# Fewer matmul signals in a graph layer: which matmuls signal, who waits for them, and wider column rings

## Chip, cores and metric

The kernel runs on one core of one Trainium2 chip. The time is device time in microseconds, median of three runs. The profile is of one separate execution.

## The reference

A graph transformer layer on N = 6250 nodes with F = 256 features and E = 106250 edges (50000 random pairs in both directions and a self loop for each node):

```python
xn = layernorm(x)
# gnn: twice  out = segment_mean(segment_mean((h @ W)[src], dst)[dst], src) + b, with prelu between
x = x + gnn(xn, edges, W1, b1, W2, b2, a) + mix(xn, Wqkv, Wout, bout)   # linear attention, 8 heads of 64
x = x + ffn(layernorm(x), ...)                                           # 8 experts, top 2, 256 -> 512 -> 256
```

Each segment mean takes for each edge the row of one end (1 KB), sums the rows by the other end, and divides by the count.

## The kernel before

Every segment sum is a pass over the edges, sorted by target block of 128 nodes (`NB` = 49 blocks) and padded to `NC` = 880 chunks of 128 edges. There are four passes (p = 0 to 3), each of `TURNS` = 55 turns of `U` = 16 chunks. In each chunk:

- ACT copies the row numbers of four chunks (`IB` = 4) to `idxb` (`row_numbers`, L616), after it has waited for `s_mm`, the matmuls of the same four slots one turn before.
- POOL issues one indirect DMA a chunk (`gather_pass`, L492) into one of 16 slots of `gbuf`. It waits for `idxb` every four chunks and for `s_mm` of its slot each time; `settle` before each is a semaphore instruction of POOL.
- PE (`product_pass`, L1281) multiplies the one-hot matrix of the chunk's targets (`ohg`) with the gathered rows into one of four PSUM banks (`AB` = 4). It waits for the gather (`s_g`) and for the bank (`s_acc`), and each matmul signals `s_mm`. The operands are fp32, and the trace shows two weight loads and two matmuls for one.
- DVE adds the bank to the accumulator of the chunk's block (`add_chunk`, L916) and signals `s_acc`; twice a turn it makes the one-hots of eight chunks (`one_hots`, L921), after `s_mm`.

The edges are sorted on the chip, once by dst (o = 0) and once by src (o = 1). In a sort, each of `EC` = 832 columns of edges (one edge per partition) becomes two one-hots on DVE (`sort_column`: `ohc` of 880 and `ohs` of 128, L839 and L840), two scaled copies on ACT (`ohv`, L606 and L607), and four f16 matmuls of 128x440 on PE (L1249), which accumulate in PSUM banks 0 to 3. The rings `ohc`, `ohs` and `ohv` hold four columns, and the last of the four matmuls of each column signals `s_used`, for which DVE waits before it fills a slot again (L838). Sort 0 does its first 384 columns by 384 indirect DMAs of POOL (`scatter`, L501) and its last 448 on DVE, ACT and PE, beside DVE's counting and placing for sort 1. Sort 1's 832 columns go beside pass 0, one for each chunk: DVE makes column k + 3 (`LEAD`), then the add of chunk k; PE does chunk k, then column k.

Beside pass 1 runs the attention's key and value part (`kv_body`, L1306 and L1296, one of 49 blocks a turn), beside pass 2 its output (`mix_body`, L1343). Between passes DVE divides by the counts and SP stores the next table. After pass 3 come the norm, the router and the experts. The order of the instructions on each engine is written out by hand, so each engine is a queue in which a waiting instruction holds all behind it.

Of the kernel before, what the change touches and what calls it, by code (L numbers as in the profile page):

```python
# [17 lines left out]
P = 128  # L18
# [30 lines left out]
def gps_layer(nc, x, src, dst, gnn_w1, gnn_b1, gnn_w2, gnn_b2, gnn_a, wqkv, wout, bout,  # L49
# [25 lines left out]
    LEAD = 3  # L75
# [19 lines left out]
    with ctx:  # L95
# [51 lines left out]
        def carve(base, sizes):  # L147

            views, at = {}, 0
            for name, (shape, dt) in sizes.items():  # L150
# [9 lines left out]
                if len(shape) == 3:  # L160
# [16 lines left out]
            "fa0": ((EC,), f32), "fb0": ((EC,), f32), "ohc": ((4, NC), f16), "ohs": ((4, P), f16),  # L177
            "ohv": ((8, P), f16), "unp": ((NC,), i32)})
# [9 lines left out]
        ohc, ohs, ohv = r["ohc"], r["ohs"], r["ohv"].rearrange("p (k f) n -> p k f n", f=2)  # L188
# [21 lines left out]
                    for at in (0, KT * 2 * INNER + 2 * PAIRS * F)]  # L210
# [37 lines left out]
        s_oh, s_ohs, s_used, s_sorted, s_idx = [[sem(f"{n}{o}") for o in range(2)]  # L248
                                                for n in ("s_oh", "s_ohs", "s_used", "s_sorted", "s_idx")]
# [198 lines left out]
        def _(pool):  # L448
# [70 lines left out]
            pool.wait_ge(s_wkv, 1)  # L519
# [57 lines left out]
        def _(act):  # L577
# [25 lines left out]
            def sort_column(o, i, k):  # L603
                c = i * U + k
                act.wait_ge(s_oh[o], (i - sort_from[o]) * U + (k + 1))
                A(ohv[:, k % 4, 0, :], ohs[:, k % 4, :], ACT.Copy, scale=field_a[o][:, ds(c, 1)])  # L606
                A(ohv[:, k % 4, 1, :], ohs[:, k % 4, :], ACT.Copy, scale=field_b[o][:, ds(c, 1)]).then_inc(s_ohs[o], 1)  # L607
# [115 lines left out]
        def _(dve):  # L723
# [194 lines left out]
            def one_hots(p, i, h):  # L918

                dve.wait_ge(s_mm[p], i * U + (8 * h + 8))  # L920
# [23 lines left out]
            def inverse(p):  # L944
                dve.wait_ge(s_acc[p], NC + AB)
# [77 lines left out]
            dve.wait_ge(s_acc[3], NC + AB)  # L1023
# [174 lines left out]
        def _(pe):  # L1198
# [13 lines left out]

            def count(o):
# [4 lines left out]
                MM(PS[:, bank, 64:64 + NB], ones[:, :], rowtot[:, 0:NB], start=True, stop=True).then_inc(s_cnt[o], 1)  # L1218
# [20 lines left out]
            def open_sort(o):  # L1239
                zero = [MM(PS[:, 2 * f + h, 0:HC], z16[:, :], iota_c[:, 0:HC], start=True, stop=False)  # L1240
                        for f in range(2) for h in range(2)]
                for m in zero:
                    m.then_inc(s_used[o], 1)

            def sort_column(o, i, k):
                pe.wait_ge(s_ohs[o], (i - sort_from[o]) * U + (k + 1))
                for f in range(2):
                    for h in range(2):
                        m = MM(PS[:, 2 * f + h, 0:HC], ohv[:, k % 4, f, :], ohc[:, k % 4, h * HC:(h + 1) * HC],  # L1249
                               start=False, stop=False)  # L1250
                m.then_inc(s_used[o], 1)

            def close_sort(o):
                for f in range(2):
                    for h in range(2):
                        m = MM(PS[:, 2 * f + h, 0:HC], z16[:, :], iota_c[:, 0:HC], start=False, stop=True)
                m.then_inc(s_sorted[o], 1)
# [13 lines left out]
            def product_pass(p, start, end, body=None):  # L1271
                if start == 0:
                    pe.sem_inc(s_mm[p], U)
                    pe.sem_inc(s_acc[p], AB)
                with pe.Fori(start, end) as i:
                    for k in range(U):
# [3 lines left out]
                        pe.wait_ge(s_acc[p], i * U + (k + 1))  # L1280
                        MM(PS[:, 4 + k % AB, 0:FC], ohg[:, k, :], gbuf[:, k, :], start=True, stop=True).then_inc(s_mm[p], 1)  # L1281
# [17 lines left out]
            def kv_body(i, k):  # L1299
                if k in (3, 5):  # L1300
# [4 lines left out]
                    for kt in range(KT):  # L1305
                        m = MM(PS[:, h, :], mx["xt"][:, kt, :], mx["wkv"][:, kt, h * INNER:(h + 1) * INNER],  # L1306
# [160 lines left out]
```

## Time and profile before

| | us |
|---|---|
| median of 3 runs | 6714.9 |
| lowest, highest | 6711.88, 6718.19 |
| span of the profiled execution, first to last instruction | 8262.6 |

The profiled execution is far longer than the timed ones. Nothing is given of it outside its span. In its views "idle before <- X" names what ended a wait; "remote" and "another core or an unknown queue" mean that the profile has no record of the update that ended it; DVEq is DVE's sequencer (register and semaphore instructions).

### The profile page before, as it was taken

What the parts mean: (1) busy time and instruction counts of PE and PEld (TensorE: products, weight loads), DVE (VectorE), ACT (ScalarE), POOL (GpSimd) and SP (SyncE); (2) the same over time, 40 slices, a digit from 0 to 9 for tenths busy, and PEclk for the clock granted to TensorE, in tenths of its full rate; (3) what the DMA queues carried; (4) which work ended last, traced back from release to release, by engine and by line L of the source; (5) the groups of instructions that cost most, each with busy time, mean ns of one, the idle gap of its engine ahead of it and who ended that gap; (6) DMA issues with size and microseconds to landing.
All of it is one profiled execution on the core that took longest, in us unless ns stands there. A gap on an engine that the chain in (4) does not pass through costs nothing. (4 is left out here: it accounts for less than half of the span.)

```text
span 8262.6 us, 93487 instructions
## 1 busy us (share of the span) xinstructions
PE 4799.4 (58%) x16274; PEld 2762.7 (33%) x16275; DVE 3919.4 (47%) x9146; ACT 1396.4 (17%) x4207; POOL 4241.7 (51%) x4243
## 2 busy tenths in 40 slices
PE   3111776666666664666666355555456555554896
PEld 2000333333333332434443233333232322334564
DVE  8411995455445444444444444444433333366323
ACT  2100553333333330000000000000000000000242
POOL 0467003444444445666666466666667666632342
PEclk6555997778777786777776667776666666666898
DMA  4000001222222224333333334444543333331114
GB/s 166 14 0 0 2 0 51 60 60 60 60 60 60 58 61 116 88 91 90 90 92 87 98 113 116 118 115 114 123 135 91 88 90 89 89 76 38 39 62 132
DMA packets 330989, 639.10 MB, mean 77 GB/s; under 512 B 81808, under 2 KB 201444, under 8 KB 330448
## 3 DMA queue, kind: packets, MB, share of 16 engines
q0 software_dynamic: 191808, 490.67, 22.1%
q1 hardware_dynamic: 131396, 140.16, 5.2%
q10 hardware_dynamic: 7756, 7.97, 0.3%
q8 instruction: 8, 0.13, 0.0%
q14 instruction: 21, 0.17, 0.0%
HBM read 551.49 MB, written 87.01 MB: 77 GB/s over the span
## 5 line engine op out<-in xcount | busy, mean ns | idle before, releaser
L492 POOL DMA_INDIRECT gbuf<-table,idxb x3520 | 3508.1, 997 | 2884.0 <-ACT idxb L616 1692.0
L1281 PE MATMUL PS<-gbuf,ohg 128*128 128x257 f32 x7040 | 2732.1, 511 | 1755.0 <-issue 1004.0
L916 DVE TENSOR_TENSOR acc<-acc,PS 128x257 f32 x3520 | 1482.8, 421 | 2506.0 <-remote 964.2
L1281 PEld LDWEIGHTS PS<-gbuf,ohg 128*128 128x128 f32 x7040 | 1520.2, 242 | 2883.1 <-issue 1688.3
L1249 PE MATMUL PS<-region 128*128 128x440 f16 x5120 | 1272.6, 383 | 1159.3 <-ACT region L607 774.6
L1249 PEld LDWEIGHTS PS<-region 128*128 128x128 f16 x5120 | 502.1, 104 | 1779.0 <-ACT region L607 926.6
L616 ACT COPY idxb<-idx 128x4 int32 (+1 forms) x884 | 167.7, 191 | 3323.2 <-PE PS L1281 1960.6
L839 DVE TENSOR_SCALAR region<-iota_c,acc 128x880 f16<-128x880 f16 x835 | 395.0, 473 | 703.3 <-remote 571.5
L921 DVE TENSOR_TENSOR ohg<-iota,dl 128x1024 f32<-128x1024 f16 x444 | 545.0, 1227 | 81.5 <-issue 55.1
L606 ACT ACTIVATE region<-region,acc 128x128 f16<-128x128 f16 x835 | 335.2, 401 | 1230.0 <-DVE region L840 983.5
L501 POOL DMA_INDIRECT scattered_d<-acc x384 | 369.8, 963 | 142.7 <-issue 129.1
L839 DVE TENSOR_SCALAR region<-iota_c,region 128x880 f16<-128x880 f16 x448 | 216.7, 484 | 471.1 <-remote 432.4
L607 ACT ACTIVATE region<-region,acc 128x128 f16<-128x128 f16 x835 | 322.0, 386 | 0.0
L606 ACT ACTIVATE region<-region 128x128 f16<-128x128 f16 x448 | 177.5, 396 | 750.9 <-DVE region L840 478.5
L782 DVE TENSOR_TENSOR_SCAN region<-region,small 128x832 f32<-128x832 f16 x112 | 220.2, 1966 | 7.0
L573 POOL DMA_INDIRECT ye_d<-gbuf,fs x108 | 106.3, 984 | 221.5 <-ACT gbuf L710 205.5
L840 DVE TENSOR_SCALAR region<-iota_h,acc 128x128 f16<-128x128 f16 x835 | 211.7, 254 | 0.0
L1419 PE MATMUL PS<-region,ohg 128*128 x436 | 207.8, 600 | 0.0
L1442 PE MATMUL PS<-acc,gbuf 128*128 x864 | 204.1, 379 | 0.0
L1306 PE MATMUL PS<-region 128*128 128x512 f32 x392 | 196.9, 627 | 0.0
L1442 PEld LDWEIGHTS PS<-acc,gbuf 128*128 128x128 f32 x864 | 164.4, 190 | 68.1 <-issue 51.6
L607 ACT ACTIVATE region<-region 128x128 f16<-128x128 f16 x448 | 172.8, 386 | 0.0
(262 smaller groups left out, 3094.0 us busy)
## 6 DMA issues: line engine op xcount, KB each, us to landing
gbuf<-table,idxb POOLq DMA_INDIRECT x3520
table<-acc SPq DMA_DIRECT2D x21, 896.0 KB, 6.7
region<-xt_d SPq DMA_DIRECT2D x98, 128.0 KB
gbuf<-ye_d SPq DMA_DIRECT2D x12, 1024.0 KB, 7.9
xpad_d<-acc SPq DMA_DIRECT2D x1, 6272.0 KB, 20.0
xn_d<-acc SPq DMA_DIRECT2D x49, 128.0 KB, 1.7
xt_d<-acc SPq DMA_DIRECT2D x49, 128.0 KB, 1.7
table<-acc SPq DMA_DIRECT2D x49, 128.0 KB, 1.7
```

The source lines that it names most:

```text
L492: gp.indirect_dma_start(gbuf[:, k, 0:F], None, tables[p], bass.IndirectOffsetOnAxis(idxb[:, k:k + 1], 0)).then_inc(s_g[k], 16)
L501: gp.indirect_dma_start(scattered_d, bass.IndirectOffsetOnAxis(ln["places"][:, h, k:k + 1], 0), ln["edges"][:, h, k:k + 1], None).then_inc ...
L606: A(ohv[:, k % 4, 0, :], ohs[:, k % 4, :], ACT.Copy, scale=field_a[o][:, ds(c, 1)])
L607: A(ohv[:, k % 4, 1, :], ohs[:, k % 4, :], ACT.Copy, scale=field_b[o][:, ds(c, 1)]).then_inc(s_ohs[o], 1)
L782: link.mark(V.tensor_tensor_scan(run, oh16[:, k, :], oh16[:, k, :], base[:, ds(b, 1)], ALU.add, ALU.bypass))
L839: TS(ohc[:, k % 4, :], iota_c[:, :], chunk_of[o][:, ds(c, 1)], None, ALU.is_equal)
L840: TS(ohs[:, k % 4, :], iota_h[:, :], slot_of[o][:, ds(c, 1)], None, ALU.is_equal).then_inc(s_oh[o], 1)
L916: TT(a, a, PS[:, 4 + k % AB, 0:FC], ALU.add).then_inc(s_acc[p], 1)
L921: TT(ohg[:, 8 * h:8 * h + 8, :], iota_1[:, :].unsqueeze(1).broadcast_to([P, 8, P]), dl[p % 2][:, ds(i * U + 8 * h, 8)].unsqueeze(2).broadc ...
L1249: m = MM(PS[:, 2 * f + h, 0:HC], ohv[:, k % 4, f, :], ohc[:, k % 4, h * HC:(h + 1) * HC], start=False, stop=False)
L1281: MM(PS[:, 4 + k % AB, 0:FC], ohg[:, k, :], gbuf[:, k, :], start=True, stop=True).then_inc(s_mm[p], 1)
L1442: m = MM(PS[:, 6 + k % 2, 0:F], fe["hT"][:, k % 2, t * P:(t + 1) * P], fa_["w2"][:, ds(es[k], 1), t, :].rearrange("p a f -> p (a f)"), sta ...
```

## The change

Of each two chunks (`GP` = 2) only the last matmul signals `s_mm`. In sort 0, one column in four (`SG` = 4) signals `s_used`; in sort 1 none does, and DVE no longer waits there (the adds' waits keep the order). POOL waits once per four gathers, for the adds `s_acc` of the four slots one turn before, in place of `s_mm` each time; ACT's copies of row numbers wait for `s_acc` too; `one_hots` waits for neither. PE waits for the banks once per pair. The column rings hold eight columns and `ohc`, `ohs` are separate for the two sorts; sort 1 leads by six columns. Single signals of PE elsewhere stand on a drain instruction behind the matmul. The setting of the ones in `gbuf` waits for the end of sort 0.

```diff
+    GP = 2
+    RING = 8
+    SG = 4
-    LEAD = 3
+    LEAD = 6
...
@@ gather_pass (POOL)
                         if k % IB == 0:
                             pool.wait_ge(s_idxb[p], i * (U // IB) + (k // IB + 1))
-                        pool.wait_ge(s_mm[p], i * U + (k + 1))
-                        settle(pool)
+                            pool.wait_ge(s_acc[p], i * U + (k + IB))
+                            settle(pool)
...
-            pool.wait_ge(s_wkv, 1)
+            pool.wait_ge(s_sorted[0], 1)
             gp.memset(gbuf[:, :, F:FC], 1.0).then_inc(s_zero, 1)
...
@@ row_numbers (ACT)
-                act.wait_ge(s_mm[p], i * U + (IB * h + IB))
+                act.wait_ge(s_acc[p], i * U + (IB * h + IB))
...
@@ sort_column (DVE)
-                dve.wait_ge(s_used[o], (i - sort_from[o]) * U + (k + 1))
-                TS(ohc[:, k % 4, :], iota_c[:, :], chunk_of[o][:, ds(c, 1)], None, ALU.is_equal)
-                TS(ohs[:, k % 4, :], iota_h[:, :], slot_of[o][:, ds(c, 1)], None, ALU.is_equal).then_inc(s_oh[o], 1)
+                if o == 0 and k % SG == 0:
+                    dve.wait_ge(s_used, (i - SC_FROM) * (U // SG) + (k // SG + 1))
+                TS(ohc[o][:, k % RING, :], iota_c[:, :], chunk_of[o][:, ds(c, 1)], None, ALU.is_equal)
+                TS(ohs[o][:, k % RING, :], iota_h[:, :], slot_of[o][:, ds(c, 1)], None, ALU.is_equal).then_inc(s_oh[o], 1)
...
@@ add_chunk and one_hots (DVE)
-                dve.wait_ge(s_mm[p], i * U + (U + k + 1))
-                dve.wait_ge(s_acc[p], i * U + (k + AB))
+                if k % GP == 0:
+                    dve.wait_ge(s_mm[p], i * (U // GP) + (k // GP + 1))
+                dve.wait_ge(s_acc[p], i * U + (U + k))
...
-                dve.wait_ge(s_mm[p], i * U + (8 * h + 8))
...
@@ PE
+            def signal(semaphore):
+
+                pe.drain().then_inc(semaphore, 1)
...
-                m.then_inc(s_used[o], 1)
+                if o == 0 and k % SG == SG - 1:
+                    m.then_inc(s_used, 1)
...
-                        pe.wait_ge(s_acc[p], i * U + (k + 1))
-                        MM(PS[:, 4 + k % AB, 0:FC], ohg[:, k, :], gbuf[:, k, :], start=True, stop=True).then_inc(s_mm[p], 1)
+                        if k % GP == 0:
+                            pe.wait_ge(s_acc[p], i * U + (U + k + GP - AB))
+                        m = MM(PS[:, 4 + k % AB, 0:FC], ohg[:, k, :], gbuf[:, k, :], start=True, stop=True)
+                        if k % GP == GP - 1:
+                            m.then_inc(s_mm[p], 1)
...
@@ kv_body, and in the same way count, close_sort, dots' last and mix_body
                     if h == 1:
-                        m.then_inc(s_kv, 1)
+                        signal(s_kv)
```

## Rows read from the trace of the kernel before

**Rows 1.** The page: busy time of each engine.
```profile
PE 4799.4 (58%) x16274; PEld 2762.7 (33%) x16275; DVE 3919.4 (47%) x9146; ACT 1396.4 (17%) x4207; POOL 4241.7 (51%) x4243
```

**Rows 2.** Windows: span; busy PE, PEld, DVE, ACT, POOL; PE clock, DMA, GB/s.
```profile
830.00:1283.00 453.00, 323.28 (x1552) 137.35 (x1552) 447.24 (x1049) 251.31 (x779) 5.25 (x2) 0.97 0.00 1
1283.00:3156.00 1873.00, 1228.80 (x5076) 683.95 (x5076) 915.25 (x2639) 597.38 (x1883) 851.70 (x880) 0.79 0.23 61
3199.00:4551.00 1352.00, 870.75 (x2543) 530.34 (x2543) 633.20 (x1376) 102.21 (x315) 887.53 (x881) 0.73 0.33 90
4641.00:5946.00 1305.00, 742.94 (x1934) 428.62 (x1934) 541.33 (x1122) 41.77 (x216) 873.30 (x880) 0.69 0.41 112
5983.00:7275.00 1292.00, 739.51 (x1749) 383.29 (x1749) 491.18 (x984) 41.97 (x217) 894.37 (x880) 0.65 0.35 98
7275.00:8262.00 987.00, 681.58 (x2754) 490.04 (x2754) 460.71 (x1311) 238.03 (x490) 304.09 (x264) 0.80 0.22 69
```

**Rows 3.** Timeline, a column of sort 0 beside the scatter.
```profile
341.86 0.39 ACT L607 ACTIVATE region<-region 128x128 f16<-128x128 f16 x1
342.30 1.65 PE L1249 MATMUL PS<-region 128*128 128x440 f16 x4 [7.59 <-issue]
349.30 0.96 POOL L501 DMA_INDIRECT scattered_d<-acc  x1 [0.30 <-issue]
350.46 0.45 DVE L839 TENSOR_SCALAR region<-iota_c,region 128x880 f16<-128x880 f16 x1 [8.19 <-remote]
```

**Rows 4.** Line L501: durations in ns, first and last start.
```profile
L501 POOL DMA_INDIRECT scattered_d<-acc x384: 952/958/1225, 289.8 to 822.1; - x192
```

**Rows 5.** Windows of L839 alone: DVE busy (x columns), PE clock.
```profile
285.00:300.00 15.00, 3.86 (x8) 0.66 0.02 2
300.00:830.00 530.00, 28.10 (x56) 0.50 0.02 0
```

**Rows 6.** Waits between 830 and 1283 us: total, times, longest.
```profile
PEld PS L1240 <- DVE idx L862: 14.3, 1, 14.3
```

**Rows 7.** Timeline, gathers of passes 0 and 2: start, duration, idle before.
```profile
1307.07 0.95 POOL L492 DMA_INDIRECT gbuf<-table,idxb  x1 [0.30 <-issue]
5644.60 0.95 POOL L492 DMA_INDIRECT gbuf<-table,idxb  x1 [0.30 <-issue]
```

**Rows 8.** Waits in pass 0.
```profile
POOL gbuf L492 <- ACT idxb L616: 1211.1, 102, 447.9
DVE region L839 <- remote: 571.5, 100, 7.3
```

**Rows 9.** Pass 0: timeline of PE and DVE, and the window 1293 to 1297.
```profile
1293.74 0.60 PE L1281 MATMUL PS<-gbuf,ohg 128*128 128x257 f32 x2
1294.92 0.60 PE L1281 MATMUL PS<-gbuf,ohg 128*128 128x257 f32 x2
1296.53 0.91 PE L1249 MATMUL PS<-region 128*128 128x440 f16 x4
1308.55 0.45 DVE L839 TENSOR_SCALAR region<-iota_c,acc 128x880 f16<-128x880 f16 x1 [8.70 <-issue]
1293.00:1297.00 4.00, 4.00 (x22) 2.60 (x21) 0.62 (x2) 0.69 (x2) 2.84 (x3) 1.00 0.36 102
```

**Rows 10.** Timeline of DVE, pass 0 without waits, one-hots, adds of pass 2.
```profile
1313.12 0.42 DVE L916 TENSOR_TENSOR acc<-acc,PS 128x257 f32 x1
1313.97 0.42 DVE L916 TENSOR_TENSOR acc<-acc,PS 128x257 f32 x1
1315.67 1.22 DVE L921 TENSOR_TENSOR ohg<-iota,dl 128x1024 f32<-128x1024 f16 x1
5653.91 0.42 DVE L916 TENSOR_TENSOR acc<-acc,PS 128x257 f32 x1 [0.21 <-DVE acc L916]
```

**Rows 11.** Chain of waits in pass 3: start, us, what.
```profile
6631.96 0.06 DVEq L916
6636.13 0.71 DVEq L913
```

More of the change, by code:

```diff
@@ L247, in gps_layer @@
         s_bwd, s_bwr = [[sem(f"{n}{o}") for o in range(2)] for n in ("s_bwd", "s_bwr")]
-        s_oh, s_ohs, s_used, s_sorted, s_idx = [[sem(f"{n}{o}") for o in range(2)]
-                                                for n in ("s_oh", "s_ohs", "s_used", "s_sorted", "s_idx")]
+        s_oh, s_ohs, s_sorted, s_idx = [[sem(f"{n}{o}") for o in range(2)] for n in ("s_oh", "s_ohs", "s_sorted", "s_idx")]
+        s_used = sem("s_used")
         s_stat, s_sd, s_ln, s_xn, s_xt, s_xtc, s_t1, s_t1c, s_lnd, s_lnfree, s_xpad = [
@@ L944, in inverse @@
             def inverse(p):
-                dve.wait_ge(s_acc[p], NC + AB)
+                dve.wait_ge(s_acc[p], NC + U)
                 link(TS(inv[:, :], accs[p % 2][:, :, F], 1.0, None, ALU.max))
@@ L1022, in _ @@
             acc_pass(3, 0, TURNS)
-            dve.wait_ge(s_acc[3], NC + AB)
+            dve.wait_ge(s_acc[3], NC + U)
             V.memset(z16[:, 0:1], 0.0).then_inc(s_fin, 1)
@@ L1217, in count @@
                 MM(PS[:, bank, 0:NB], lower[:, :], rowtot[:, 0:NB], start=True, stop=True)
-                MM(PS[:, bank, 64:64 + NB], ones[:, :], rowtot[:, 0:NB], start=True, stop=True).then_inc(s_cnt[o], 1)
+                MM(PS[:, bank, 64:64 + NB], ones[:, :], rowtot[:, 0:NB], start=True, stop=True)
+                signal(s_cnt[o])
             pe.wait_ge(s_wkvc, 2)
@@ L1239, in open_sort @@
             def open_sort(o):
-                zero = [MM(PS[:, 2 * f + h, 0:HC], z16[:, :], iota_c[:, 0:HC], start=True, stop=False)
-                        for f in range(2) for h in range(2)]
-                for m in zero:
-                    m.then_inc(s_used[o], 1)
+                for f in range(2):
+                    for h in range(2):
+                        MM(PS[:, 2 * f + h, 0:HC], z16[:, :], iota_c[:, 0:HC], start=True, stop=False)
+                if o == 0:
+                    pe.sem_inc(s_used, RING // SG)
             def sort_column(o, i, k):
@@ L1255, in close_sort @@
                     for h in range(2):
-                        m = MM(PS[:, 2 * f + h, 0:HC], z16[:, :], iota_c[:, 0:HC], start=False, stop=True)
-                m.then_inc(s_sorted[o], 1)
+                        MM(PS[:, 2 * f + h, 0:HC], z16[:, :], iota_c[:, 0:HC], start=False, stop=True)
+                signal(s_sorted[o])
             pe.wait_ge(s_bw[0], 1)
@@ L1272, in product_pass @@
                 if start == 0:
-                    pe.sem_inc(s_mm[p], U)
-                    pe.sem_inc(s_acc[p], AB)
+                    pe.sem_inc(s_acc[p], U)
                 with pe.Fori(start, end) as i:
@@ L1319, in _ @@
             dots()
-            MM(PS[:, 2, :], z16[:, :], iota_c[:, 0:512], start=False, stop=True, skip_group_check=True).then_inc(s_dots, 1)
+            MM(PS[:, 2, :], z16[:, :], iota_c[:, 0:512], start=False, stop=True, skip_group_check=True)
+            signal(s_dots)
             product_pass(1, NB, TURNS)
@@ L1342, in mix_body @@
                     for kt in range(KT):
-                        m = MM(PS[:, 0, 0:F], mx["xt"][:, kt, :], gmat[:, kt, :], start=kt == 0, stop=kt == KT - 1)
-                    m.then_inc(s_mix, 1)
+                        MM(PS[:, 0, 0:F], mx["xt"][:, kt, :], gmat[:, kt, :], start=kt == 0, stop=kt == KT - 1)
+                    signal(s_mix)
             pe.sem_inc(s_mix, 1)
```

19 lines of the change are left out of this document (10 added, 9 removed).

## Prediction

> **What bounds the kernel now.** I read the page first: no engine is busy for more than 58% of the span [rows 1], so no engine's work explains it; it is made of waits. The windows by stage then show where time goes [rows 2]: four passes of 880 gathers each, of 1873, 1352, 1305 and 1292 us, are 5822 of 8262 us. The reader is to see that POOL's busy time is nearly the same in all four (852 to 894 us) while their length is not.
>
> The timeline gives POOL's own pace: a gather takes 0.95 us and the next one starts 0.30 us later, 1.25 us apart, with nothing to wait for [rows 7]. 880 of them are 1100 us, 20.0 us a turn. So every pass exceeds what POOL needs, by 773, 252, 205 and 192 us. The waits of pass 0 say what POOL lacks there: row numbers from ACT, 1211 us (448 of which lie before the first gather) [rows 8]. ACT copies them when PE's matmuls have signalled.
>
> Next I asked whether PE is late or its signal. In the timeline of sort 0, PE has its four matmuls of a column issued by about 343.9 us, and DVE, which only waits for a free slot of four, goes on at 350.46, after 8.19 us idle, with "remote" as releaser; ACT to PE takes 0.05 us in the same place [rows 3]. In pass 0, PE issues without a gap up to 1297.4, and then stands; DVE's next column starts at 1308.55, after 8.70 us idle [rows 9]. POOL goes on issuing through both. What is late is the update from a matmul to its waiter, and it is late while POOL issues indirect DMAs; from 830 to 1283 us, where POOL does nothing, DVE is busy 447 of 453 us [rows 2]. This is an inference: the releaser has no record.
>
> **The sum against the profiled execution.** Without late signals, the start would be as follows. Only 64 of the 448 columns are done by 830 us [rows 5]. From there to 1283 us DVE does the last 384 with counting and placing in 453 us, 1.18 us each [rows 2]; all 448 would take 528 us from 290 on, to 818. The scatter goes on to 823 whatever DVE does [rows 4], and about 14 us of unpacking follow [rows 6], with a few for the read back: first gather at 840 instead of 1283, 443 us less. So:
>
> 840 (start) + 4 x 1100 (gathers) + 43 + 90 + 37 (between passes) + 987 (rest) = 6397 us.
>
> The profiled span, 8263, is 1866 above it. The median of the timed runs, 6714.9, is 318 above it. The two differ by 1548 us for the same program. So at most about a sixth (318 of 1866) of these stalls exists in a timed run. That the profile itself stretches the kernel is seen on DVE's sequencer as well: in pass 3 the same kind of register instruction takes 0.06 us and, 4 us later, 0.71 [rows 11]. I therefore take the shape of the stalls from the trace and their size from the median. If sort 0 had none of the 318 us, the passes of a timed run would be 7% above POOL's pace (318 / 4400).
>
> **The change part by part.**
>
> Signals removed. Pass 0 loses 24 of 32 PE signals a turn, the other passes 8 of 16, sort 0 three of four. If delivery is a matter of how many, half to three quarters of the 318 us goes; if none of the 318 us is late signals, 0 goes. Both ends stay: 0 and 318. I take 60%, because pass 0 and sort 0, which lose three quarters, hold 1216 of the profile's 1866 us, and because a late signal of a pair still holds two chunks. That is -191 us.
>
> The signals' cost to PE's own issue: at the full clock, 2.4 GHz, a chunk and a column with their two signals repeat every 1.18 us, PE busy 4.00 of 4 us [rows 9], 18.8 us a turn, under POOL's 20.0. So it is covered by POOL: 0.
>
> A page of the Trainium skill, "TensorE: Matmul & The Clock Gate", section "The cost: per-tile semaphore tail", says that increments on consecutive matmuls serialize at about 26 ns each and that one on the last is enough. By it 2928 fewer signals (4800 before, 1872 after) are an estimated 77 us at most, if none were covered; the sum would then be 6641 instead of 6527. The trace shows no gap of that kind, and the page has no delay of 8 us.
>
> Fewer instructions on POOL: a `settle` and a register wait leave three of four gathers. The scatter, which has neither between its DMAs, has the same 0.30 us between two [rows 3, 7]. Worth 0; if it did not hold, 3520 x 0.30 would be the far bound, and that is a rival below.
>
> Gathers and row numbers behind the adds: the longer chain is gather landed, pair of matmuls, add, copy, gather. A slot has 16 gathers of 1.25 us, 20.0 us, before it is needed; a group of four must be done after 13 of them, 16.3 us. Added is one pair's second chunk (1.25) and four adds, each with a column in pass 0, 0.85 us apart when DVE has no wait [rows 10]: 3.4 us. That leaves about 11 us for landing, matmul and signal. Cost 0 as long as a signal is no later than that; otherwise the second rival.
>
> Pairs of banks: PE waits for the two adds of the pair before last instead of a single one four back. It has one pair, 2.36 us at full clock [rows 9], for two adds with a column, 1.7 us, plus signals; the one-hots of eight chunks (1.22 us) can make PE wait [rows 10], but POOL gives 1.2 us a turn of cover. 0, at most 1 us in each of 55 turns.
>
> Drains: one in each of 49 turns of passes 1 and 2. PE is idle 481 and 562 us there [rows 2], which hides them; without cover, 98 x 0.6 us (the time of one chunk's matmuls [rows 9]) is 59 us. 0. Three more columns ahead of pass 0: 3 x 0.85 = 3 us on the path. Memset of the ones after sort 0: under the 14 us of unpacking, 0.
>
> Sum: 6714.9 - 191 + 3 = 6527, I say 6530 us. The same for the profiled execution, where signals are the larger part: between 30% and 60% of 1866 gone, a span of 7150 to 7700.
>
> **Rivals.**
>
> *Nothing to gain.* The late updates belong to the profiled execution alone, and the 318 us is something else (PE at its lower clock, gathers that land late). For: 1548 of 1866 us are known to be absent from timed runs. Against: something stretches them by 318, and the profile shows nothing else that delays POOL. Time 6718, 3 us over the median.
>
> *The adds hold the gathers.* When signals come late and together, ACT today copies four row numbers at once and POOL starts at once. After the change POOL starts only when DVE has added all four, 3.4 us later in pass 0: 55 x 3.4 = 187 us, and up to 2.5 us a turn in the others (4 x 0.63) [rows 10]. It decides from a delay of 11 us on. The trace has such waits, since POOL's stops in pass 0 are 14 us a turn (773 / 55). Against: fewer signals should be less late. In full, 6900; at half its price, 6810.
>
> *Much more.* If the timed gather is faster than the traced one, say 1.15 us, the floor is 6045 and the excess 670; 60% of that makes 6315. For: sequencers are slower under the profiler. Against: the pitch is the same with and without instructions between, which says that it is not theirs.
>
> **Numbers.** Forecast (50 to 290 us less) 0.52; nothing 0.15; adds hold the gathers 0.20; much more 0.13. The forecast's own range is 6425 to 6665. The range over all, 6340 to 6790, cuts off the far halves of the last two. A difference under 0.2% (13 us) is what a measurement of this kernel can't tell from none; so faster 0.65, same 0.15, slower 0.20.
>
> **What would show it.** In the profile after: in sort 0 beside the scatter, more than 56 columns by 830 us and the first gather well before 1283; in pass 0, fewer and shorter idle times of L839 and of POOL, a pass under 1500 us; POOL's pitch still 1.25 us. If the gap between two gathers shrinks, the term I set to 0 was wrong. If POOL waits for `s_acc` with DVE's adds running at 0.85 us each before it, the second rival holds. If the profiled span falls by hundreds of microseconds and the median does not, the first one does. The forecast fails if the 318 us isn't late signals.

## The result, and the profile after

| | before | after |
|---|---|---|
| median | 6713.4 us (4 runs) | 6779.9 us (4 runs) |
| lowest to highest | 6709.4 to 6718.2 | 6779.3 to 6783.8 |
| profiled execution, time / span | span 8262.6 | 6779.9 / 6778.1 |

The ratio is 1.0097, 95% interval [1.0083, 1.0112]: the change makes the kernel 66 us slower. The forecast was 6530 us, faster.

The profiled execution of the changed kernel is as short as its timed ones, while that of the kernel before is 1548 us longer than the timed ones. The experiments below say why: the kernel takes 6711 to 6715 us on some chips (kind A here) and 8251 to 8443 us on others (kind B), timed or profiled alike. By its length the result above is of kind A, the trace of the kernel before of kind B. So [rows 2] and what follows lie stage by stage beside each other, but the difference is mostly that of the chips. (A kind is a name for what a chip showed during these runs. One chip of kind B was met twice and was the same both times; no chip was seen in both kinds. Whether the cause lies in the chip itself isn't shown.)

The page: busy time of each engine, then the groups of POOL's gathers and DVE's one-hots (busy us, mean ns | idle before).

```profile
PE 5097.9 (75%) x16274; PEld 2646.6 (39%) x16275; DVE 3884.1 (57%) x9152; ACT 1398.4 (21%) x4213; POOL 4432.6 (65%) x4243
...
L497 POOL DMA_INDIRECT gbuf<-table,idxb x3520 | 3571.9, 1015 | 1223.5 <-issue 1008.8
...
L927 DVE TENSOR_TENSOR ohg<-iota,dl 128x1024 f32<-128x1024 f16 x444 | 541.6, 1220 | 0.0
```

Windows of the changed kernel by stage (columns as in [rows 2]): scatter and sort 0, the end of the scatter, the four passes, the rest.

```profile
290.00:500.00 210.00, 161.03 (x770) 68.47 (x771) 207.10 (x542) 125.96 (x386) 162.44 (x151) 0.98 0.02 1
500.00:800.00 300.00, 214.81 (x1032) 88.44 (x1029) 299.76 (x661) 168.22 (x511) 246.28 (x172) 1.00 0.01 0
800.00:956.00 156.00, 1.65 (x4) 0.43 (x4) 22.91 (x35) 4.32 (x16) 107.68 (x112) 0.50 0.02 3
956.00:2155.00 1199.00, 1131.61 (x5075) 603.67 (x5076) 883.21 (x2641) 594.83 (x1882) 917.21 (x880) 0.98 0.35 96
2203.00:3360.00 1157.00, 945.87 (x2537) 489.72 (x2537) 626.30 (x1372) 102.71 (x315) 889.15 (x881) 0.78 0.37 104
3452.00:4583.00 1131.00, 856.84 (x1940) 405.58 (x1940) 539.32 (x1127) 41.96 (x217) 863.10 (x881) 0.72 0.46 130
4622.00:5791.00 1169.00, 980.06 (x1744) 420.19 (x1744) 481.75 (x979) 41.97 (x217) 901.15 (x880) 0.56 0.37 108
5791.00:6778.00 987.00, 683.78 (x2759) 489.48 (x2758) 464.42 (x1315) 238.24 (x490) 304.21 (x264) 0.79 0.22 69
```

Read POOL's column (the fifth engine). In [rows 2] a pass was 192 to 773 us longer than 1100 us because POOL stood; here the passes are only 31 to 99 us longer, and POOL's busy time is higher than the 832.5 us that 880 gathers of 0.946 us take (the median of e18's gathers). The missing time lies inside the gathers. The timeline shows where (start, duration, [idle before]):

```profile
5030.80 1.22 DVE L927 TENSOR_TENSOR ohg<-iota,dl 128x1024 f32<-128x1024 f16 x1
5031.21 1.64 POOL L497 DMA_INDIRECT gbuf<-table,idxb  x1 [0.30 <-issue]
```

This gather, issued while DVE makes one-hots, lasts until 0.83 us after they end (5032.85 against 5032.02), 1.64 us in place of 0.95. In pass 3 this meets two of 16 gathers in each turn. The moment that decides follows from the two durations: 0.95 - 0.83 = 0.12 us after the gather's start. In the trace of pass 3, one-hots are running at that moment in 109 of the 880 gathers. Each of these ends 0.83 us after the one-hots (to 0.03 us), or after its own 0.95 us where that is later. The other 771 take 0.95 us, and none of them more than 1.05.

The scatter is lengthened too. Line L506 (durations in ns, first and last start, to be laid beside [rows 4]):

```profile
L506 POOL DMA_INDIRECT scattered_d<-acc x384: 953/977/2484, 289.1 to 930.5; - x192
```

Windows of that line alone, ahead of sort 1's placing, beside it, and behind it:

```profile
289.00:400.00 111.00, 80.03 (x82) 0.97 0.02 1
410.00:810.00 400.00, 311.82 (x205) 0.99 0.01 0
810.00:932.00 122.00, 86.87 (x91) 0.50 0.02 0
```

The timeline, DVE's wait for the end of the scatter:

```profile
936.06 7.74 DVE L858 TENSOR_SCALAR idx<-ohg 128x880 int32<-128x880 int32 x1 [131.88 <-DMA ohg<-scattered_d]
```

Sort 0's columns are now done in time: DVE makes 438 of them between 300 and 830 us, where [rows 5] has 56. But beside them DVE scans and selects for sort 1, and there a scatter DMA takes 1.52 us on the mean (311.82 / 205) in place of 0.98 before and 0.95 after. All but 1 us of this excess lies in DMAs that ran beside a scan (1.94 us) or a predicated copy (1.08 us) of that selection, not in those beside sort 0's columns alone. The scatter ends 108 us later than in [rows 4], and DVE, done at about 804 us, waits 132 us for it. The first gather is issued at 955.9 us.

By stage the span is 956 (start) + 1199 + 1156 + 1130 + 1169 (passes, first to last gather) + 48 + 93 + 40 (between) + 987 (rest) = 6778 us. The forecast's floor had 840 + 4400 + 170 + 987 = 6397. The 381 us between them are: 116 up to the first gather (108 of it the stretched scatter; the forecast's 17 us from the scatter's end to the first gather are 25), 254 in the passes, 11 between them. In the passes, POOL's DMAs that last longer than 0.946 us make 242 us (3571.9 - 4 x 832.5), and 14 us are waits in pass 0 (e4 below). No late signal of PE appears among them.

### The profile page after: what moved, and what is told of

Its sections match the earlier page's. It is cut to its first block, busy times and chain, and to the rows that moved or that the text cites. A ratio compares the mean times of both kernels' runs of the same rounds, so it can differ in the third digit from the quotient of the medians.

```text
span 6778.1 us, 84181 instructions
## 1 busy us (share of the span) xinstructions
PE 5097.9 (75%) x16274; PEld 2646.6 (39%) x16275; DVE 3884.1 (57%) x9152; ACT 1398.4 (21%) x4213; POOL 4432.6 (65%) x4243
## 4 chain that ended last, share of the span: by engine, by line
POOL 25%; PE 19%; issue 18%; DMA 13%; DVE 8%; DVEq 1%; ACT 1%; POOLq 0%; ACTq 0%; SPq 0%; PEldq 0%
POOL gbuf L497 24%; DMA gbuf<-table,idxb 12%; PE PS L1294 9%; DVE acc L923 3%; PE PS L1435 3%; PE PS L1458 3%; PE PS L1415 1%; PE PS L1451 1%; DMA gbuf<-ye_d 1%; PE PS L1321 1%; ACT idxb L621 1%; PE PS L1261 1%; PE PS L1398 0%; DVE gbuf L1144 0%; DVE fs L1051 0%
## 5 line engine op out<-in xcount | busy, mean ns | idle before, releaser
L497 POOL DMA_INDIRECT gbuf<-table,idxb x3520 | 3571.9, 1015 | 1223.5 <-issue 1008.8
L1294 PE MATMUL PS<-gbuf,ohg 128*128 128x257 f32 x7040 | 3133.3, 551 | 801.7 <-DMA gbuf<-table,idxb 577.4
L1294 PEld LDWEIGHTS PS<-gbuf,ohg 128*128 128x128 f32 x7040 | 1419.4, 245 | 2462.9 <-DMA gbuf<-table,idxb 1058.7
L1261 PE MATMUL PS<-region 128*128 128x440 f16 x3328 | 755.8, 350 | 0.0
L506 POOL DMA_INDIRECT scattered_d<-acc x384 | 486.5, 1267 | 133.6 <-issue 114.4
L1261 PE MATMUL PS<-gbuf,region 128*128 128x440 f16 x1792 | 374.7, 353 | 202.2 <-ACT region L612 199.3
L1261 PEld LDWEIGHTS PS<-region 128*128 128x128 f16 x3328 | 326.1, 98 | 268.6 <-issue 1.4
L1261 PEld LDWEIGHTS PS<-gbuf,region 128*128 128x128 f16 x1792 | 155.9, 98 | 420.6 <-ACT region L612 313.9
L611 ACT ACTIVATE region<-gbuf,region 128x128 f16<-128x128 f16 x448 | 177.8, 397 | 282.4 <-DVE gbuf L846 281.9
L845 DVE TENSOR_SCALAR gbuf<-iota_c,region 128x880 f16<-128x880 f16 x448 | 208.3, 465 | 0.5 <-DVE region L752 0.4
```

Source lines behind the costliest of these rows:

```text
L497: gp.indirect_dma_start(gbuf[:, k, 0:F], None, tables[p], bass.IndirectOffsetOnAxis(idxb[:, k:k + 1], 0)).then_inc(s_g[k], 16)
L506: gp.indirect_dma_start(scattered_d, bass.IndirectOffsetOnAxis(ln["places"][:, h, k:k + 1], 0), ln["edges"][:, h, k:k + 1], None).then_inc ...
L611: A(ohv[:, k % RING, 0, :], ohs[o][:, k % RING, :], ACT.Copy, scale=field_a[o][:, ds(c, 1)])
L845: TS(ohc[o][:, k % RING, :], iota_c[:, :], chunk_of[o][:, ds(c, 1)], None, ALU.is_equal)
L1261: m = MM(PS[:, 2 * f + h, 0:HC], ohv[:, k % RING, f, :], ohc[o][:, k % RING, h * HC:(h + 1) * HC], start=False, stop=False)
L1294: m = MM(PS[:, 4 + k % AB, 0:FC], ohg[:, k, :], gbuf[:, k, :], start=True, stop=True)
```

## The experiments

The runs fell on six chips. Time of each against the kernel before on the same chip:

| run | what | kind, time of before | time | ratio, 95% |
|---|---|---|---|---|
| e1 | before again | B, 8442.9 | 8442.2 | 0.9997 [0.9987, 1.0007] |
| e2 | column part alone | B, 8442.9 | 8377.4 | 0.9921 [0.9905, 0.9938] |
| e3 | chunk part alone | B, 8442.9 | 8496.5 | 1.0061 [1.0045, 1.0078] |
| e4 | changed, gates on matmuls | B, 8442.9 | 8350.9 | 0.9892 [0.9867, 0.9916] |
| e5 | changed again | B, 8251.1 | 8177.3 | 0.9905 [0.9875, 0.9936] |
| e6 | column part | B, 8251.1 | 8244.1 | 0.9987 [0.9972, 1.0001] |
| e7 | chunk part | B, 8251.1 | 8365.9 | 1.0152 [1.0119, 1.0184] |
| e8 | before, one execution | B, 8260.7 | 8255.4 | |
| e9 | column part | B, 8260.7 | 8248.4 | 0.9987 [0.9977, 0.9997] |
| e10 | chunk part | B, 8260.7 | 8372.4 | 1.0138 [1.0122, 1.0155] |
| e11 | changed, one-hots later | B, 8427.7 | 8389.9 | 0.9957 [0.9944, 0.9970] |
| e12 | chunk part | B, 8427.7 | 8476.9 | 1.0055 [1.0035, 1.0076] |
| e13 | before, one execution | B, 8427.7 | 8415.1 | |
| e14 | changed, more DVE work | B, 8256.5 | 8403.2 | |
| e15 | changed, one-hots left out | B, 8256.5 | 8298.8 | 1.0053 [1.0028, 1.0077] |
| e16 | before, one execution | B, 8256.5 | 8260.5 | |
| e17 | chunk part | A, 6714.8 | 6773.0 | 1.0085 [1.0052, 1.0119] |
| e18 | column part | A, 6710.9 | 6736.3 | 1.0038 [1.0024, 1.0053] |

**Before again, and the changed kernel again (e1, e5, e8, e13, e16).** No edit.

> The kernel before, unchanged, to see whether the long profiled execution (8263 us beside timed runs of 6713) comes again, and the spans and clocks of its timed runs. If the stretching belongs to the profiled execution of this kernel: profile again above 8000 us, timed 6713 (ratio 0.998 to 1.002). If it was chance: a span near 6712, whose passes and first gather then show where the changed kernel lost 66 us.

> The changed kernel, unchanged. The previous four runs fell on a chip on which the kernel before takes 8443 us in timed runs too, with PE's signals late as in its first profile. If this call falls on a chip where the kernel before takes 6713: ratio 1.008 to 1.011. If it falls on a late one: the sum of the two parts measured there, 0.992 and 1.006, is 0.998; if the adds holding the gathers cost only there, 0.995 to 1.000.

> The kernel before, for a profile on a chip whose signals are in time. There: span near 6712, and the table of stages then shows against the changed kernel (first gather 956, passes 1199, 1156, 1130 and 1169 us) where the 66 us are. Theory 1: first gather earlier than 956 by 50 us or more, since DVE is held a little beside the scatter. Theory 2: passes shorter by 50 us or more in total. On a late chip: above 8000 again.

> The kernel before, unchanged, for its trace. If the chip is one on which it takes 6713 us, its stages answer where the change's 66 us arise: theory start, a first gather at about 890 to 900 us and four passes of the changed kernel's length (1199, 1156, 1130, 1169); theory passes, a first gather near 956 us and passes shorter by 16 us each. If the chip is one on which it takes 8250 to 8440 us, the stages of the trace before: first gather near 1280, passes 1873, 1352, 1305, 1292.

> The kernel before, unchanged, for its trace on this chip. Where it takes 6713 us: theory start, a first gather at about 890 to 900 us and four passes of the changed kernel's length (1199, 1156, 1130, 1169); theory passes, a first gather near 956 us and passes that sum to about 66 us less. Where it takes 8250 to 8440 us: first gather near 1280, passes 1873, 1352, 1305, 1292 within 70 us each.

On four chips, one of them met twice, the kernel before took 8251 to 8443 us in timed executions too, which neither alternative of e1 had foreseen. So the long trace of before came from such a chip and not from the profiler. Of the three single executions, e16's passes lie within 7 us of those in [rows 2], and e13's up to 86 us off.

On kind B the changed kernel is 1% faster, more than either value expected of e5. Gathers of the kernel before, pass by pass, on e5's chip (e16; the same windows of e5 stand at e15 below):

```profile
1283.00:3153.00 1870.00, 853.23 (x880) 0.79 0.23 61
3194.00:4553.00 1359.00, 887.34 (x880) 0.74 0.32 89
4642.00:5950.00 1308.00, 877.57 (x880) 0.69 0.40 112
5985.00:7275.00 1290.00, 885.04 (x880) 0.65 0.34 98
```

The change's first gather comes 14 us earlier (1269 against 1283) and its pass 0 is 137 us shorter (1733 against 1870), while passes 1 to 3 are 11, 49 and 16 us longer. By the medians that is 74 us in all where the stalls of [rows 3, 8, 9] exist in full, about 4% of the 1866 us that the prediction counted. Its timeline beside the scatter shows that the stall of [rows 3] is still there, only in larger pieces:

```profile
410.33 0.45 DVE L845 TENSOR_SCALAR gbuf<-iota_c,region 128x880 f16<-128x880 f16 x1 [40.59 <-remote]
```

And a window of its columns alone (to be laid beside [rows 5]):

```profile
300.00:830.00 530.00, 32.27 (x67) 0.56 0.02 0
```

DVE waits 40 us for one signal of four columns, where it waited 8 to 9 us for one of each. With a quarter of the signals it makes 67 columns by 830 us; the kernel before makes 54 on the same chip (e16), 56 in [rows 5] and 66 on another chip (e1). So on kind B the stall hardly depends on the number of signals. That it goes with the number of columns is an inference, since the releaser has no record.

**One part at a time on kind B (e2, e3, e6, e7, e9, e10, e12).** The column part alone keeps the chunks' loop of before, with all its waits (the edit against the changed kernel, in part):

```diff
-                            pool.wait_ge(s_acc[p], i * U + (k + IB))
-                            settle(pool)
+                        pool.wait_ge(s_mm[p], i * U + (k + 1))
+                        settle(pool)
...
-                        m = MM(PS[:, 4 + k % AB, 0:FC], ohg[:, k, :], gbuf[:, k, :], start=True, stop=True)
-                        if k % GP == GP - 1:
-                            m.then_inc(s_mm[p], 1)
+                        pe.wait_ge(s_acc[p], i * U + (k + 1))
+                        MM(PS[:, 4 + k % AB, 0:FC], ohg[:, k, :], gbuf[:, k, :], start=True, stop=True).then_inc(s_mm[p], 1)
...
```

The chunk part alone keeps the rings of four with a signal for each column, and has neither the drains nor the later memset (how it differs from the changed kernel, in part):

```diff
-    RING = 8
-    SG = 4
-    LEAD = 6
+    LEAD = 3
...
-                if o == 0 and k % SG == SG - 1:
-                    m.then_inc(s_used, 1)
+                m.then_inc(s_used[o], 1)
...
```

> The column part alone (rings of 8, one signal in four columns or none, lead of 6, drains), the chunk signals and waits as before. Theory 1 (the loss lies in sort 0: DVE, no longer held by signals, runs beside the scatter and slows POOL's DMAs there, which end later): ratio 1.008 to 1.015, first gather near 955 us. Theory 2 (the loss lies in the passes, from adds that hold the gathers and from pairs): ratio 0.995 to 1.002.

> The chunk part alone (one signal for two chunks, gathers and row numbers behind the adds), columns as before. Theory 1: ratio 0.995 to 1.002. Theory 2: ratio 1.008 to 1.015, with passes longer than POOL's 1100 us by waits for adds.

> The column part alone again, for the chip where signals are in time. Theory 1 (loss in sort 0, DVE against POOL's scatter): ratio 1.008 to 1.015. Theory 2 (loss in the passes): 0.995 to 1.002. On a late chip 0.992 again.

> The chunk part alone again. Theory 1: ratio 0.995 to 1.002. Theory 2: 1.008 to 1.015. On a late chip 1.006 again.

> The column part alone. Theory 1: ratio 1.008 to 1.015 on a chip in time. Theory 2: 0.995 to 1.002. On a late chip 0.992 to 0.999.

> The chunk part alone. Theory 1: ratio 0.995 to 1.002 on a chip in time. Theory 2: 1.008 to 1.015. On a late chip 1.006 to 1.015.

> The chunk part alone (pairs' signals of one matmul in the four passes, gathers and index copies behind the adds; the sort's columns as before). Where the kernel before takes 8250 to 8440 us it measured 1.006 to 1.015. Theory start: DVE's faster columns stretch POOL's scatter, and the 66 us of the change arise before the first gather; then this part alone is within 0.998 to 1.003 where the kernel before takes 6713. Theory passes: the 66 us arise in the four passes; then this part alone is 1.007 to 1.013.

On kind B the column part gains 0.1 to 0.8% and the chunk part loses 0.6 to 1.5%, while both together gain 1% (e5). The first repeats, e6 and e7, missed what was expected of them (0.9987 for 0.992, 1.0152 for 1.006). So the parts don't add up there, and these runs say nothing of kind A.

**Are the adds what holds the gathers? (e4)** The changed kernel, with POOL and ACT waiting for the pairs' matmuls again:

```diff
-                            pool.wait_ge(s_acc[p], i * U + (k + IB))
+                            pool.wait_ge(s_mm[p], i * (U // GP) + (k + IB) // GP)
...
-                act.wait_ge(s_acc[p], i * U + (IB * h + IB))
+                act.wait_ge(s_mm[p], i * (U // GP) + (IB * h + IB) // GP)
...
```

> The changed kernel, but POOL and ACT wait for the pairs' matmuls and not for DVE's adds. Theory 2 in the form 'the adds hold the gathers': ratio near 1.000 instead of 1.010, that is 60 us less than the changed kernel. Theory 1: no difference to the changed kernel, ratio 1.008 to 1.011.

0.9892 with these gates, 0.9905 with those of the change on another chip: no difference that the intervals separate. Of kind A there is no such run, but its trace answers the question. The waits of the changed kernel's pass 0 on POOL:

```profile
POOL gbuf L497 <- issue: 242.8, 762, 1.9
POOL gbuf L497 <- DVE acc L923: 28.0, 92, 0.3
POOL gbuf L497 <- ACT idxb L621: 23.0, 26, 12.0
```

The 92 waits put down to the adds are 0.3 us each, which is the gap that stands there anyway (92 x 0.30 = 28). But POOL also waits for the row numbers, whose copy on ACT waits for adds. The timeline of pass 0 has this at the fifth gather of a turn:

```profile
1003.87 0.19 ACT L621 COPY idxb<-idx 128x4 int32 x1
1004.94 0.95 POOL L497 DMA_INDIRECT gbuf<-table,idxb  x1 [0.59 <-issue]
```

The last add before the copy ends at 1003.24. The gap is 0.59 us instead of 0.30, and such longer gaps stand at that place in 37 of the 55 turns of pass 0. With one more they are 14 us above 0.30, and in passes 1 to 3 there are none. The chunk part has the same (15 us, e17). The column part, whose copies wait for matmuls, has a single one of 0.7 us (e18). So the adds do hold the gathers, by 13 to 14 us in pass 0 and not more.

**One-hots at another place (e11).**

```diff
-                        if k == 1:
+                        if k == 2:
...
-                        if k == 9:
+                        if k == 10:
```

> The changed kernel with the one-hots of a chunk written after the pair's second add (places 2 and 10 of the chunk's loop in place of 1 and 9), so that DVE's 1.22 us instruction no longer falls between a pair's two adds. Theory phase: in the changed kernel the one-hots fall at a fixed place against POOL's gathers and stretch them; moving them changes which gathers are stretched and by how much. Where the kernel before takes 6713 us, the changed kernel's gathers carry 242 us of stretched duration over the four passes; if the phase makes them, this run takes 60 to 200 us less than 6780, ratio 0.975 to 1.00. Where the kernel before takes 8250 to 8440 us, where the change itself measured 0.9905, a ratio of 0.985 to 0.995. Rival, that any place of the one-hots costs the same: ratio 1.010 where the kernel before takes 6713, 0.9905 elsewhere.

0.9957, just above what I expected for kind B. POOL's gathers were busy 3497.8 us, 168 above 3520 x 0.946; in e5 it was 191 (the four rows below). Inconclusive: on kind B the stalls in front of the gathers decide, and there is no run of it on kind A.

**Which DVE instructions stretch POOL's DMAs? (e14)** Ahead of sort 0's first column DVE gets work that waits for no other engine, in three blocks (comments added; `link.wait(14)` waits for DVE's own instruction 14 places before, and the other blocks have 2 and 7):

```diff
+            with dve.Fori(0, 11) as i:      # 16 times each: the two column forms
...
+                    link.wait(14)
+                    link.mark(TS(ohc[0][:, k % RING, :], iota_c[:, :], chunk_of[0][:, k:k + 1], None, ALU.is_equal))
+                    link.mark(TS(ohs[0][:, k % RING, :], iota_h[:, :], slot_of[0][:, k:k + 1], None, ALU.is_equal))
...
+            with dve.Fori(0, 11) as i:      # 9 times: the one-hots' form, in gbuf
...
+                    link.mark(TT(gbuf_flat[...], iota_1[:, :].unsqueeze(1).broadcast_to([P, 8, P]),
+                                 iota_h[:, 0:8].unsqueeze(2).broadcast_to([P, 8, P]), ALU.is_equal))
...
+            with dve.Fori(0, 16) as i:      # 32 times: an add with both operands in SBUF
...
+                    link.mark(TT(gbuf_flat[...], run[:, 0:FC], run[:, FC:2 * FC], ALU.add))
...
```

> The changed kernel with work added that waits for no TensorE: before sort 0's first column DVE runs 352 column instructions (176 pairs of the two column forms), then 99 of the one-hots' form (128x1024), then 512 additions of the adds' size (128x257, both operands in SBUF), each block about 100 to 140 us long, while POOL scatters. Theory, DVE's instructions stretch POOL's indirect DMAs: the scatter's DMAs in the columns' block have a mean duration of 1.1 to 1.5 us, in the one-hots' block 1.4 us or more, and in the adds' block something between 0.96 and 1.3; and the scatter ends later than 822 us on any chip. Rival, it is something else of the faster sort (ScalarE, TensorE, the DMA queues): the DMAs stay at 0.96 us on the mean in all three blocks, and the scatter ends at 822 us.

Windows of the scatter's DMAs alone (POOL busy, count) beside the three blocks, the third up to 804 us:

```profile
289.00:629.00 340.00, 236.22 (x244) 0.50 0.02 0
629.00:740.00 111.00, 90.42 (x49) 0.50 0.01 0
742.00:804.00 62.00, 45.62 (x44) 0.50 0.02 0
```

The timeline of POOL in the third block:

```profile
807.45 107.81 POOL L506 DMA_INDIRECT scattered_d<-acc  x1 [2.16 <-issue]
```

Mean durations: 0.97 us beside the column instructions (236.22 / 244), 1.85 us beside the one-hots' form (90.42 / 49, most of them 1.96), 1.04 us beside the SBUF adds, until one DMA starts at 807.45 and ends at 915.3, 0.8 us after the last of the adds: DVE shut POOL out for 107.8 us. Of my theory one half holds and one falls: DVE does it, but the scatter isn't lengthened by the column instructions. What lengthens it has two operands in SBUF: the one-hots, in sort 0 the scan and the predicated copy, here the adds. The column instructions have one tensor operand, the kernel's own adds have one in PSUM.

Beside gathers the column instructions aren't quite harmless. In pass 0 of the changed kernel, on kind A, 100 gathers that meet no one-hots take 1.05 to 1.20 us, each with the large column instruction running 0.12 us after its start:

```profile
1011.29 0.43 DVE L845 TENSOR_SCALAR region<-iota_c,acc 128x880 f16<-128x880 f16 x1
1011.37 1.18 POOL L497 DMA_INDIRECT gbuf<-table,idxb  x1 [0.30 <-DVE acc L923]
```

Each of the 100 ends 0.83 us after that instruction, to 0.02 us. Why a gather meets this and a scatter not isn't known.

The Trainium skill, "SBUF — State Buffer", section "SBUF: two separate sides", states a rule of this kind: a vector operation in a two-port mode and a GpSimd operation exclude each other for a whole instruction, and one with two SBUF inputs excludes a GpSimd operation that reads SBUF. It says of the two-port mode that the descriptors of a POOL-issued DMA can't be written meanwhile; of two-input operations it doesn't say so. The trace shows that these hold up indirect DMAs as well (1.85 us on the mean, once 107.8 us). The same section gives "blocked until DVE-end + ~115 ns" for a DMA under a vector copy. A gather here ends 0.83 us after the one-hots, and no run shows whether the two figures mean the same moment.

**Without the one-hots (e15).** Passes 1 to 3 of the changed kernel leave the one-hots out and use those of pass 0; a small instruction keeps the signals:

```diff
+                if p:
+                    TS(ohg[...0:1], ohg[...0:1], 0.0, None, ALU.add).then_inc(s_ohg[p], 1)
+                    return
```

> The changed kernel without the one-hots of passes 1 to 3 (it leaves this computation out: a small instruction on 128x8 elements stands in for each, and the one-hots of pass 0 are used again). Theory, the one-hots stretch the gathers: in passes 1 to 3 the gathers' duration above 0.946 us sums to under 60 us in place of 100 to 160, and pass 0 keeps its own. The time falls by no more than these, ratio to the kernel before 0.95 to 0.985 where that takes 8250 to 8440 us; where it takes 6713, 6780 less 120 to 160 us, ratio 0.985 to 0.992. Rival, the adds stretch the gathers as much: the sums stay within 20 us of the changed kernel's.

Windows of the gathers alone, four passes of e5, the changed kernel on the same chip:

```profile
1269.00:3002.00 1733.00, 893.75 (x880) 0.85 0.24 66
3048.00:4418.00 1370.00, 867.11 (x877) 0.76 0.31 88
4510.00:5867.00 1357.00, 869.37 (x876) 0.70 0.39 108
5895.00:7201.00 1306.00, 883.93 (x880) 0.66 0.34 97
```

The same of e15:

```profile
1280.00:3013.00 1733.00, 895.16 (x880) 0.85 0.24 66
3060.00:4498.00 1438.00, 828.38 (x875) 0.77 0.30 84
4590.00:5962.00 1372.00, 833.32 (x879) 0.70 0.39 107
6000.00:7341.00 1341.00, 833.17 (x880) 0.67 0.33 95
```

Above 0.946 us a gather, passes 1 to 3 have 130 us with one-hots (867.11 - 877 x 0.946, and so on) and 3 us without; pass 0, which keeps its own, has 61 and 63. So all of the gathers' stretching in passes 1 to 3 comes from the one-hots, and none from the adds. Yet the kernel did not take less time, though a ratio of 0.95 to 0.985 had been expected. It took about 120 us more than the changed one (8298.8 against 8177.3, both on this chip): its passes 1 to 3 are 68, 15 and 35 us longer, all of it POOL standing. On kind B a faster gather is paid back by stalls. Why more than back isn't known.

**The parts on kind A (e17, e18).** The edits are those of e3 and e2.

> The chunk part alone, with the sort's columns as before, so that its stretch up to the first gather is that of the kernel before. Where the kernel before takes 6713 us: theory start, a first gather at about 890 to 900 us and a ratio of 0.998 to 1.003; theory passes, a first gather within 10 us of 956 us and a ratio of 1.007 to 1.013. Where it takes 8250 to 8440 us, ratio 1.006 to 1.015 as measured.

> The column part alone (rings of 8, one signal for 4 columns); its four passes have the chunks of the kernel before. Where the kernel before takes 6713 us, the first gather stands at 955 us as in the chunk part alone, and theory passes says: ratio 0.998 to 1.002; the gathers' duration above 0.946 us sums to about 180 us over the four passes in place of 231 in the chunk part alone and 242 in the changed kernel, spread over more places of the turn than 5 and 13. Rival, the gathers wait in the passes of the chunk part for something the trace doesn't show as their duration: the sum stays at 230 us or more here too, and the passes are shorter in their gaps. Where it takes 8250 to 8440 us, ratio 0.992 to 0.999 as measured.

Windows of the gathers alone (POOL busy, count), four passes of the chunk part:

```profile
954.00:2144.00 1190.00, 906.44 (x880) 0.97 0.35 96
2190.00:3347.00 1157.00, 888.38 (x880) 0.78 0.37 104
3440.00:4577.00 1137.00, 867.77 (x880) 0.71 0.46 129
4615.00:5782.00 1167.00, 898.18 (x880) 0.55 0.38 108
```

Its first gather in the timeline:

```profile
954.69 1.01 POOL L493 DMA_INDIRECT gbuf<-table,idxb  x1 [11.10 <-ACT idxb L617]
```

The same windows of the column part:

```profile
955.00:2120.00 1165.00, 895.72 (x880) 0.98 0.36 98
2167.00:3313.00 1146.00, 876.91 (x880) 0.78 0.37 106
3403.00:4569.00 1166.00, 896.39 (x880) 0.71 0.45 126
4606.00:5752.00 1146.00, 876.82 (x880) 0.56 0.39 110
```

Its first gather, and one-hots in pass 3, in the timeline:

```profile
955.31 1.01 POOL L497 DMA_INDIRECT gbuf<-table,idxb  x1 [12.00 <-ACT idxb L621]
...
5028.99 0.95 POOL L497 DMA_INDIRECT gbuf<-table,idxb  x1 [0.30 <-issue]
5029.19 1.22 DVE L927 TENSOR_TENSOR ohg<-iota,dl 128x1024 f32<-128x1024 f16 x1
5030.24 0.99 POOL L497 DMA_INDIRECT gbuf<-table,idxb  x1 [0.30 <-issue]
```

The first gather comes at 954.7 us with the old columns and at 955.3 and 955.9 with the new ones: the change gains and loses nothing there, since the scatter sets it, and "theory start" falls. The loss is in the passes. The chunk part costs 58 us (1.0085, as "theory passes" said), the column part 25 us, which nothing had foreseen (1.0038 where 0.998 to 1.002 was expected). Together that is 83, which agrees with the measured 66 within the intervals.

Within the passes, gathers above 0.946 us sum to

| | pass 0 | 1 | 2 | 3 | sum | POOL's waits in the passes |
|---|---|---|---|---|---|---|
| changed | 86 | 57 | 30 | 69 | 242 | 14 |
| chunk part (e17) | 74 | 56 | 35 | 66 | 231 | 15 |
| column part (e18) | 63 | 44 | 64 | 44 | 216 | 1 |

(waits: what the gaps between gathers have above 0.305 us, summed; a sum of about 180 had been expected for e18, and 230 or more by its rival.)

The single passes differ by up to 34 us, but passes 1 to 3 together hardly do. From the first gather's start to the last's they are 3454, 3455 and 3451 us in the order of the table. What separates the changed kernel from the column part is pass 0, with 1199, 1188 and 1163 us. Of those 36 us, 13 are the waits for row numbers (e4), and the rest are longer gathers. Sorted by what DVE ran beside them, the gathers of pass 0 that meet no one-hots, only sort 1's columns, are 25, 31 and 7 us above 0.946; those that meet one-hots 61, 43 and 56. So, beside the column part, the chunks' new loop costs its time in pass 0, by waits and by gathers that meet columns, and not through the one-hots of the other passes.

The last three lines of the column part's timeline show how one-hots can cost nothing: they begin 0.20 us after a gather, past the 0.12 us, and that one takes 0.95 us and the next 0.99. In the changed kernel they begin 0.41 us ahead of one, and it takes 1.64. The places in the order of instructions are nearly the same; the phase between DVE and POOL is not. One gather in each turn that is hit at the bad phase costs 55 x 0.58 to 0.69 = 32 to 38 us a pass, which is the size by which single passes differ.

The kernel before has no trace from kind A. If its other stages are those of the three traces, its passes are by subtraction 6713.4 - 1.8 (time less span) - 955 - 181 - 989 (the last three terms are the same in the three traces of kind A to within 4 us in sum) = 4587 us, against 4654, 4643 and 4614 in the three traces. The difference to the changed kernel, 67 us, is the change's loss.

## Why the prediction was wrong

**The step that failed: "take the shape of the stalls from the trace and their size from the median", and with it "the 318 us is late signals".** I took the profiled execution for a stretched copy of the timed one. It was a whole execution on a chip where the kernel takes 8250 us and more; in the traces from chips of the other kind, the stalls of [rows 3, 8, 9] don't exist. That DVE's sequencer was once slower [rows 11] was no evidence for a slow profiler. What the 318 us holds on kind A: 115 us up to the first gather (955 in place of 840, nearly all of it the stretched scatter) and, by the subtraction above, 187 us in passes (4587 - 4400), 11 between them and 2 in the rest, 315 of 318; the other 3 are the time outside the span and the median's own change from 6714.9 to 6713.4. Nothing in it is seen to be a late signal, so the term of -191 us was 0.

**"If delivery is a matter of how many" failed as well.** Where the late signals exist, on kind B, 2928 of 4800 signals fewer took 74 us off (e5), 4% of 1866 and not 30 to 60%. The forecast span of 7150 to 7700 us for a profiled execution is 8185 there. The signs that the prediction named (more than 56 columns, an early first gather, a pass under 1500 us) are all in the trace after, but through its chip: the chunk part has its first gather at 954.7 us with the old columns.

**"The scatter goes on to 823 whatever DVE does" failed too.** [rows 4] showed a scatter beside a DVE that mostly stood; with DVE at work it ends at 931. The inference used a row from a state that the same argument removed.

**"POOL's pitch still 1.25 us"** held for 0.95 + 0.30 where DVE is quiet, and failed on the mean: 4654 / 3520 = 1.32 us.

**The costs set to 0 on POOL.** The gap between gathers stayed 0.30 us without `settle`, as said. The gathers and row numbers behind the adds cost the 14 us of waits in pass 0 instead of 0. The pairs of banks: PE waits for adds 167 times for 85 us in pass 0, and no wait of POOL beyond those 14 us is seen to come of it. The signals' serializing had no visible value: with fewer of them neither part got faster on kind A, so nothing of the 77 us estimated from the Trainium skill's "TensorE: Matmul & The Clock Gate" shows.

**The rival that ended on the other side was right in sign and mostly wrong in cause.** "The adds hold the gathers" forecast 6810 to 6902, with up to 187 us in pass 0; the adds hold them by 14 us. "Nothing to gain" had the right premise, that the 318 us is something else, and forecast 6718. It missed what no term of mine contained: that a gather lasts longer when it meets certain instructions of DVE, and that new waits and columns change how often it does.

**What stays open.** The 40 us between the changed kernel and the column part are shown in the traces: 26 in longer gathers and 13 in waits, nearly all in pass 0. The 25 us of the column part are not: the kernel before was never traced on kind A, so how long its gathers are there, and in which pass it is shorter, isn't known. Moving the one-hots at will on a chip of kind A wasn't tried, nor the changed kernel there with its old gates. And why chips differ by 23 to 26% isn't known.

## What to carry to other kernels

Before a profile is scaled to a median, ask whether it comes from the same condition: a profiled span 23% over the timed one is a reason to explain the difference first, and a forecast built on its stalls is worth little until that is done. When POOL's indirect DMAs set the pace, list what DVE runs with two SBUF operands beside them: here each such instruction lengthened a DMA by up to about its own duration, and shorter waits elsewhere bought nothing. What a change of 1% is made of shows only pass by pass: single passes moved by 34 us with the phase, and the part of the loss that could be traced sat in one of the four.

## What the runs showed of the hardware that was not expected

The same program takes 6711 to 6715 us on some chips and 8251 to 8443 us on others, and a change can have opposite signs on them (0.9905 and 1.0097). The difference isn't only in PE's signals. In e14 DVE's column instructions, which wait for no other engine and only for a signal of DVE's own instruction 14 places before, run 0.32 us apart at first and later up to 1.40 us apart:

```profile
446.09 0.26 DVE L896 TENSOR_SCALAR gbuf<-iota_h,region 128x128 f16<-128x128 f16 x1 [0.95 <-issue]
446.80 0.45 DVE L895 TENSOR_SCALAR gbuf<-iota_c,region 128x880 f16<-128x880 f16 x1 [0.45 <-DVE gbuf L896]
448.19 0.26 DVE L896 TENSOR_SCALAR gbuf<-iota_h,region 128x128 f16<-128x128 f16 x1 [0.95 <-issue]
```

The one-hots' block behind them ran at its own pace (110.65 of 111 us busy) and the adds' at 0.34 us, so it isn't a fixed rate of DVE either. And a stream of short DVE instructions can lock POOL out for as long as it lasts: one indirect DMA took 107.8 us, though the 44 of the window before it, beside the same adds, took 1.04 on the mean.
